# Four-layer attention kernel: which PSUM banks layer 0's scores use, two squares without a wait between, and layer 3's stages at new places

## The reference, cut to what matters

```python
def step(s, rkvw):
    r_t, k_t, v_t, w_t = rkvw
    a = k_t[..., :, None] * v_t[..., None, :]
    out = jnp.einsum('bhi,bhij->bhj', r_t, u * a + s)
    s = a + w_t[..., :, None] * s
    return (s, out)
...
var = jnp.mean(jnp.square(x), axis=-1, keepdims=True)
return x * jax.lax.rsqrt(var + EPS) * w
```

## Time and profile before

| | us |
|---|---|
| median of 3 runs | 1815.32 |
| lowest and highest | 1812.19, 1816.52 |
| the profiled execution's own time | 1816.85 |
| its span | 1815.0 |

### The profile page before, as it was taken

The page is one execution under the profiler, slowest core; times in us unless marked ns, Lnnn a source line. Parts: engine busy times, 40 slices in busy tenths (PEclk is TensorE's granted clock), DMA queues, the critical chain, the costliest instruction groups (busy, mean ns, idle before and its releaser), DMA issues.

```text
span 1815.0 us, 35492 instructions
## 1 busy us (share of the span) xinstructions
PE 1621.3 (89%) x13831; PEld 1053.9 (58%) x13831; DVE 1221.7 (67%) x2259; ACT 936.1 (52%) x1922; POOL 770.9 (42%) x882
## 2 busy tenths in 40 slices
PE   5888898899998899998998989889899889988856
PEld 3666556675565655655566655667456565565534
DVE  3743569755786558845689456975579665884496
ACT  4455545555645545556455564555564554555313
POOL 5532248603584046721477024860358404672000
PEclk8999999998999999999999999999999999999978
DMA  6001014210241004310061101421024100520060
GB/s 194 1 2 38 1 18 56 32 36 7 33 58 37 19 1 57 40 30 19 1 72 26 30 20 18 55 34 34 7 35 56 37 20 1 62 36 1 13 90 17
DMA packets 75924, 60.84 MB, mean 34 GB/s; under 512 B 39264, under 2 KB 60912, under 8 KB 75760
## 3 DMA queue, kind: packets, MB, share of 16 engines
q1 hardware_dynamic: 58000, 47.99, 18.3%
q10 hardware_dynamic: 17216, 10.55, 2.1%
q0 software_dynamic: 544, 0.03, 0.0%
HBM read 20.28 MB, written 4.19 MB: 13 GB/s over the span
## 4 chain that ended last, share of the span: by engine, by line
PE 66%; DVE 14%; ACT 9%; issue 5%; POOL 5%; DMA 0%; ACTq 0%; DVEq 0%; SPq 0%; POOLq 0%
PE bank L690 26%; PE bank L834 7%; PE bank L1097 6%; PE bank L1034 5%; DVE late L1409 4%; PE bank L706 3%; PE bank L1059 2%; PE bank L981 2%; ACT soft_ring L1235 2%; PE bank L967 2%; POOL soft_ring L1785 2%; PE bank L1052 2%; PE bank L943 2%; PE bank L954 1%; PE bank L774 1%
## 5 line engine op out<-in xcount | busy, mean ns | idle before, releaser
L1785 POOL TENSOR_TENSOR soft_ring<-soft_ring,seg_max 128x512 f32<-128x512 f32 x256 | 279.5, 1107 | 282.4 <-DVE seg_max L1575 281.4
L1250 ACT ACTIVATE soft_ring<-soft_ring 128x512 f32<-128x512 f32 x256 | 160.1, 625 | 188.1 <-POOL soft_ring L1785 188.0
L1409 DVE TENSOR_TENSOR_SCAN late<-late 128x520 f32<-128x520 f32 (+1 forms) x128 | 211.1, 1649 | 15.8 <-POOL late L1740 12.2
L834 PE MATMUL bank<-early 32*128 32x128 f32 (+2 forms) x1024 | 152.3, 416 | 39.1 <-ACT soft_ring L1235 37.9
L1034 PE MATMUL bank<-ident,soft_ring 128*128 128x128 f32 x1024 | 165.0, 290 | 22.8 <-ACT soft_ring L1250 17.4
L1738 POOL TENSOR_TENSOR late<-late 128x520 f32<-128x520 f32 x112 | 167.9, 1499 | 38.9 <-DVE late L1409 38.5
L1034 PEld LDWEIGHTS bank<-ident,soft_ring 128*128 128x128 f32 x1024 | 116.9, 145 | 92.8 <-ACT soft_ring L1250 44.9
L1575 DVE TENSOR_REDUCE seg_max<-soft_ring 128x8 f32<-128x512 f32 (+1 forms) x256 | 165.5, 674 | 0.2
L1751 POOL COPY late<-edge 128x8 f32<-128x8 f32 (+1 forms) x16 | 3.1, 197 | 327.2 <-DVE late L1513 279.5
L1793 POOL TENSOR_SCALAR soft_ring<-soft_ring,rden 128x256 f32<-128x256 f32 x64 | 59.3, 927 | 180.4 <-DVE rden L1537 180.4
L834 PEld LDWEIGHTS bank<-early 32*128 32x128 f32 (+1 forms) x1024 | 76.7, 192 | 90.0 <-issue 88.0
(11 more groups left out here) (327 smaller groups left out, 3482.2 us busy)
## 6 DMA issues: line engine op xcount, KB each, us to landing
late<-late SPq DMA_DIRECT2D x112, 260.0 KB, 4.4
c<-in_ctx ACTq DMA_DIRECT2D x8, 512.0 KB, 4.1
x<-in_x ACTq DMA_DIRECT2D x8, 512.0 KB, 4.9
out_x<-late SPq DMA_DIRECT2D x7, 512.0 KB, 2.9
late<-late SPq DMA_DIRECT2D x16, 130.0 KB, 3.8
early<-early SPq DMA_DIRECT2D x16, 130.0 KB, 3.6
mask<-in_mask_Bx1xSxS_ff ACTq DMA_DIRECT2D x16, 128.0 KB, 4.0
mask<-in_mask_BxS_ik SPq DMA_DIRECT2D x8, 256.0 KB, 3.5
```

The lines of the kernel that those rows point to most:

```text
L834: ins = mm(t[:, width * n:width * n + width], lhsT, rhs, start=True, stop=True)
L1250: af(soft[:, u % SOFT, :], soft[:, u % SOFT, :], ACT.Exp).then_inc(sig("exp"), 1)
L1409: nc.vector.tensor_tensor_scan(P.sj[:, n % 2, :], P.wP[:, k, :, :].rearrange("p b t -> p (b t)"), P.aj[:, n % 2, :], 0.0, ALU.mult, ALU.ad ...
L1785: tt(s, s, seg_max[:, u % SOFT, 0:segs].unsqueeze(2).broadcast_to([128, segs, 512 // segs]), ALU.subtract).then_inc(sig("sub"), 1)
```

## The change

In layer 0 the pairs p = 1 and p = 3 fill banks of the ring "turn" and not of "score". In layer 2's RMS norm ACT no longer waits for its first square before it starts the second. And most numbers of `PLACES` and `SCAN_PLACES` are others.

```diff
-            "turn": (11, 12, 5, 0),
-            "shift": (12, 15, 11, 4),
-            "maa": (15, 16, 12, 12),
-            "mix 0": (17, 29, 16, 18),
-            "mix 1": (22, 29, 20, 18),
-            "td": (29, 29, 30, 18),
+            "turn": (11, 10, 3, 0),
+            "shift": (11, 10, 11, 9),
+            "maa": (15, 15, 15, 10),
+            "mix 0": (17, 28, 18, 17),
+            "mix 1": (22, 28, 24, 28),
+            "td": (29, 28, 28, 32),
...
-            "mix 2": (35, 29, 35, 22),
-            "decay": (37, 36, 36, 23),
-            "v": (42, 37, 40, 31),
-            "mix 3": (42, 37, 40, 35),
+            "mix 2": (35, 29, 34, 33),
+            "decay": (39, 36, 37, 36),
+            "v": (42, 36, 41, 37),
+            "mix 3": (42, 36, 41, 39),
...
-            "r": (45, 43, 42, 47),
+            "r": (46, 43, 43, 50),
...
-            "bonus": (56, 49, 54, 56),
-            "center": (124, 124, 121, 113),
-            "variance": (127, 128, 122, 121),
-            "gate": (132, 130, 124, 121),
-            "project": (132, 133, 126, 127),
+            "bonus": (56, 50, 53, 54),
+            "center": (125, 125, 121, 118),
+            "variance": (127, 127, 124, 126),
+            "gate": (130, 129, 124, 126),
+            "project": (133, 133, 124, 126),
...
-            "ffn k": (135, 135, 133, 141),
-            "ffn r": (141, 145, 137, 147),
-            "ffn v": (149, 151, 148, 151),
+            "ffn k": (135, 141, 128, 138),
+            "ffn r": (138, 149, 128, 153),
+            "ffn v": (147, 154, 146, 156),
         }
         SCAN_PLACES = (
-            (64, 53, 64, 60), (64, 53, 68, 63), (64, 54, 68, 66), (64, 59, 69, 67), (72, 59, 69, 67),
-            (78, 78, 69, 67), (78, 80, 70, 67), (84, 88, 84, 70), (85, 91, 88, 89), (98, 93, 88, 89),
-            (101, 93, 100, 89), (107, 93, 105, 100), (112, 94, 108, 105), (116, 94, 109, 107), (116, 97, 114, 109),
-            (116, 107, 117, 109), (116, 109, 117, 109), (116, 111, 119, 111), (122, 114, 121, 111),
+            (63, 52, 64, 58), (63, 54, 67, 65), (64, 54, 67, 66), (65, 61, 67, 67), (71, 61, 69, 67),
+            (75, 79, 69, 67), (75, 79, 71, 67), (83, 89, 83, 67), (83, 90, 88, 85), (96, 93, 88, 89),
+            (100, 93, 100, 90), (105, 99, 106, 100), (109, 100, 108, 105), (112, 102, 109, 105), (112, 102, 115, 105),
+            (112, 106, 117, 105), (116, 107, 120, 110), (116, 110, 120, 110), (125, 115, 121, 110),
         )
...
-                def side_by_side(tiles, steps, operands):
+                def side_by_side(tiles, steps, operands, ring="score"):
 
-                    held = [fill(pe, "score", tile) for tile in tiles]
+                    held = [fill(pe, ring, tile) for tile in tiles]
...
-                        mn[HALVES[half], p, 128 * n:128 * n + 128], mm0[HALVES[half], p, :]))
+                        mn[HALVES[half], p, 128 * n:128 * n + 128], mm0[HALVES[half], p, :]), "turn" if p % 2 else "score")
...
-                                link(af(xh[:, p, :], xr[:, p, :], ACT.Square, accum_out=stats[:, p, 0:1]))
+                                ins = af(xh[:, p, :], xr[:, p, :], ACT.Square, accum_out=stats[:, p, 0:1])
+                            link(ins)
```

More of the change, by code:

```diff
@@ L478, in build @@
             "moments": (0, 0, 0, 0),
-            "normalize": (4, 12, 1, 0),
-            "turn": (11, 12, 5, 0),
-            "shift": (12, 15, 11, 4),
-            "maa": (15, 16, 12, 12),
-            "mix 0": (17, 29, 16, 18),
-            "mix 1": (22, 29, 20, 18),
-            "td": (29, 29, 30, 18),
-            "k": (32, 29, 34, 18),
-            "mix 2": (35, 29, 35, 22),
-            "decay": (37, 36, 36, 23),
-            "v": (42, 37, 40, 31),
-            "mix 3": (42, 37, 40, 35),
-            "mix 4": (43, 39, 42, 46),
-            "r": (45, 43, 42, 47),
-            "g": (49, 49, 46, 48),
-            "r u k": (50, 49, 50, 48),
-            "bonus": (56, 49, 54, 56),
-            "center": (124, 124, 121, 113),
-            "variance": (127, 128, 122, 121),
-            "gate": (132, 130, 124, 121),
-            "project": (132, 133, 126, 127),
[L500 to L503, removed]
-            "ffn k": (135, 135, 133, 141),
-            "ffn r": (141, 145, 137, 147),
-            "ffn v": (149, 151, 148, 151),
+            "normalize": (4, 5, 1, 0),
+            "turn": (11, 10, 3, 0),
[4 more added lines that the diff above has]
+            "td": (29, 28, 28, 32),
+            "k": (32, 29, 34, 33),
+            "mix 2": (35, 29, 34, 33),
+            "decay": (39, 36, 37, 36),
+            "v": (42, 36, 41, 37),
+            "mix 3": (42, 36, 41, 39),
+            "mix 4": (43, 39, 42, 50),
+            "r": (46, 43, 43, 50),
+            "g": (49, 49, 46, 50),
+            "r u k": (52, 50, 50, 50),
+            "bonus": (56, 50, 53, 54),
[3 more added lines that the diff above has]
+            "project": (133, 133, 124, 126),
+            "moments 2": (133, 133, 127, 126),
+            "normalize 2": (134, 133, 127, 134),
+            "turn 2": (134, 133, 127, 134),
+            "shift 2": (135, 137, 127, 134),
+            "ffn k": (135, 141, 128, 138),
+            "ffn r": (138, 149, 128, 153),
+            "ffn v": (147, 154, 146, 156),
         }
         SCAN_PLACES = (
[4 rows of a table removed]
[4 rows of a table added]
         )
```

## The result

The changed kernel takes 1791.69 us (median of 4 runs, 1787.11 to 1792.58), the kernel before 1815.92 beside it (1812.19 to 1817.37). The ratio is 0.9865 with a 95% interval of 0.9842 to 0.9888, so faster by 24.2 us. The prediction had 1803.0 with a range of 1790 to 1814: the sign and the range held, the size was half of what came. The forecast of the first rival, 1793, is closest; whether its mechanism is what happened is what most of the experiments are about.

The account below looks back on a forecast made before the run. TensorE was taken as the bound, so only its idle times and low-clock stretches could yield gains. Terms summed to -1.1 us a block, -7.7 in seven, -12.2 with the first block, giving 1803 us, range 1790 to 1814.

Parts of the forecast that it names:

- the first rival: Clock stays up: layer 0 gains 3.6 us and the pick 1.1, a block -2.5, 1793 us in all; chance 0.13.
- Layer 0: First scores to `x1T` in seven blocks: shorter waits gain 2.8 us each, bounds 1.7 and 3.6.
- First block: Layer 0 of the first block: ScalarE's own work becomes the chain, -4.5 us, between -2 and -7.
- Variance: MLP, seven blocks: ScalarE's variance one unit earlier makes u5 wait, +1.45 us each, bounds 1.3 and 1.6.
- Scans: The moved scan places in seven blocks: together +0.25 us each.
- (d): Scans: pick 4 moves ahead of `keys2` and waits for a row being read, +0.1 us, bounds 0 and 0.2.
- (c): Scans: picks 12 and 14 move ahead of project 6; the 0.99 us wait grows, +0.3 us, bounds 0 and 0.4.
- (a): Scans: POOL's product for n = 8 moves earlier; transposes come 0.35 us later, bounds 0 and 1.1.
- (b): Scans: pick 8 moves ahead of `lT` 1 into idle time, -0.5 us, bounds 0 and -1.1.
- The main case: Whole kernel: -1.1 us a block in seven, -12.2 with the first block, 1803 us; chance 0.54.
- Gain and stall cancel: Clock falls in every block, layer 0's 1.7 us gain is cancelled, only the first block's -4.5 remains: 1811 us; chance 0.22.
- The stall at u5 lowers the clock: MLP: low clock behind u5's wait costs 1.7 us in each of seven blocks, 1823 us; chance 0.10.

Follow-up runs that it names:

- variance_back: The changed kernel with ScalarE's variance stage at 128 again, behind the third GELU: 1785.1 us, ratio to the kernel before 0.9801-0.9852.
- scans_back: The changed kernel with the scans at their old places: 1801.6 us, ratio to the kernel before 0.9888-0.9938.
- nudge_2: The changed kernel with two extra 128x512 matmuls (1.75 us), once, behind MLP product u7 of the third group: 1796.5 us.
- each_1: The changed kernel with one extra 128x512 matmul (0.87 us) behind MLP product u7 of every group: 1805.6 us.
- waits_back_work: The changed kernel with ScalarE's variance at 128, TensorE's pick 4 at 72, and three extra 128x512 matmuls behind u7 of every group: 1816.9 us.
- banks_turn10: The kernel before with only the second and fourth score pairs in the turn ring and ScalarE's turn drain at 10: 1816.7 us.
- nudge_4: The changed kernel with four extra 128x512 matmuls (3.6 us), once, behind MLP product u7 of the third group: 1796.3 us.

## Why the prediction was right, and where its sizes were not

*Bound.* TensorE stays the bound, as forecast. That an edit can gain only in idle times and in stretches of low clock holds; by the split into busy and idle time nearly all came from the second of these, and the sum had been made of the first.

*Layer 0, forecast -2.8, upper bound -3.6.* Measured -3.65 in the fourth group. The waits are as told: the forecast had 2.2, 1.4 and 0.5, the trace has 2.38, 1.29 and 0.67, and their sum, 4.3 for 4.1, is right. The miss lies in TensorE's busy time: the forecast took 0.9 us off it for the slow pair, and it fell by 2.03, for the low clock had held the transposes behind the pair too (four in 1.11 us, now 0.63) and the 0.8 us of "slack in adding matmuls" did not exist. The runs add what the text had not: the three numbers carry one another. The banks without the drain's and the mix's new places give 0.4, the places without the banks cost 2.4.

*First block, forecast -4.5.* From first scores to `x1T` it took 27.12 us and takes 22.05: -5.1, of which 1.8 are idle time and 3.3 busy time that had run at 0.50. The size is near; the forecast had made it of ScalarE's chain and had not counted the clock.

*Variance, forecast +1.45.* u5 waits 1.35 in the place foretold, and the segment behind u3 grew by 1.49. That it is a loss agrees with variance_back, whose stall is gone. By an estimate with the drain of the Trainium skill, "ScalarE: Activation LUTs", section on what ACT_TABLE_LOAD costs, it would have been 4.2; the trace disagrees: behind both loads the next instruction starts 1.30 and 1.29 us after the load's start.

*Scans, forecast +0.25.* (d) pick 4 was mis-sized: 1.21 for 0.1, since TensorE with full clock is at the pick before VectorE's scan and add (2.13 + 0.66 us) have made its row. (c): the picks that waited 0.99 and 0.55 wait 0.53 and 1.44, +0.43 for +0.3. (a): the transposes wait 1.45, less than before, within the bounds. (b): the pick took 1.05 between the transposes and `lT` 1, at full clock. In all the segments up to `lT` 1 stay level (+0.01). scans_back, though, has 8.9 us less idle time in six groups, so by waits alone the new places of the scans cost up to 1.5 and not 0.25.

*The step that failed: the clock outside layer 0.* The main case kept every low stretch where it was and gave none a price; the first rival gave back layer 0's and the pick's, 1.4 a block. Measured, the stretch from `lT` 1 to `xnT` 1 gives 3.38 in the fourth group: 4.88 less busy time, which is the clock's, and 1.50 more idle time. That closes this group's account: -5.5 where -1.1 was forecast is 0.85 more in layer 0, 0.25 in the scans and 3.4 here. Over six groups 18 low stretches less give 26.6 us of busy time, against 8.9 more of idle time. The whole span: -6.2 in the first group (forecast -4.5; the other kernels with the new banks take 1.7 to 3.5 us longer there than this execution), -17.8 in the six (-6.6), -6.1 in the last with what layer 3 does alone behind it (-1.1), and 0.3 later at the start. By its own sign ("if low clock lies elsewhere") the forecast was wrong in its clock. That its range held is in part luck: the range reached down to 1790 for the sake of the first rival, and the reason of that rival was not enough.

*Rivals.* "The clock stays up" came, with its number nearly. Its reason, the shorter gap, is not enough: the same gap lets the clock fall with the banks alone, in nudge_2 and in the changed kernel's own second group. "Gain and stall cancel" rested on a clock that falls in every block. "The stall at u5 lowers the clock": 1.35 us at 785.18 had no low clock behind it. "A table load holds ScalarE longer": no.

*Left open.* How much of the 24 us the change would keep if its gaps came at other times isn't settled. nudge_2 and each_1 say it is not safe: 1.75 us of work once cost 4.8, 7 us in all cost 13.9. Nor is it settled why this kernel settles without low clock in 5 groups and waits_back_work with it in all; the start of the run was not varied by itself, though the executions differ in it. And the three executions of the changed kernel that were not profiled, at clocks of 0.975 to 0.981, may well have more low stretches than the table's row.

## What to carry to other kernels

Split a group's time into busy and idle time of the engine that bounds it, and the granted clock, before pricing an edit: here the idle time rose by 8.9 us, the busy time fell by 26.6, and the kernels with the least idle time (88.6 and 91.3) were not the fastest. A new buffer and a new place in a queue belong together; undo them one by one and both look bad. When a change gains through the clock, shift it by a microsecond or two and see whether the gain stays.

## What the runs showed of the hardware

Whether TensorE's clock falls behind an idle time hangs on more than its length. The same 2.38 us ahead of layer 0's first transposes stand in all eight groups of the changed kernel and of the eleven experiments that have the new banks, 96 times in the profiled executions, and low clock (0.50) followed 48 times: once in the changed kernel, seven times with the banks alone, eight times in banks_turn10, never in nudge_4. The Trainium skill, "TensorE: Matmul & The Clock Gate", section on the HAM clock gate, lets the clock follow how busy the array has lately been; that low clock begins soon behind the gaps agrees, but no row here tells why the same gap behind the same instructions goes both ways. In busy time a low stretch that lacks 1.7 us of clock cost 1.5 us here; in the kernel's time it cost less, since slower work covers waits. So a kernel with low clock shows fewer waits, and idle time alone is no measure of it.
